# Eight groups of unread TensorE products taken out of the start of a two-layer gated network

## The reference, cut to what matters

```python
x = x + jnp.tanh(g_xattn[0]) * _L0_xattn_ref(_layernorm(x, axis=-1), fside_BxS2xS2_0, ctx_1024)
x = x + jnp.tanh(g_ffn[0]) * _L0_ffn_ref(_layernorm(x, axis=-1), L0_ffn_gate_w, ...)
x = x + jnp.tanh(g_xattn[1]) * _L1_xattn_ref(_layernorm(x, axis=-1), ctx_1024, L1_xattn_Wq, ...)
x = x + jnp.tanh(g_ffn[1]) * _L1_ffn_ref(_layernorm(x, axis=-1), L1_ffn_router_w, ...)
```

```python
amax_x = jnp.max(jnp.abs(x), axis=0)
amax_w = jnp.max(jnp.abs(w), axis=0)
s = jnp.sqrt(jnp.maximum(amax_x, EPS) / jnp.maximum(amax_w, EPS))
xs = x / s
ws = w * s
x_scale = jnp.maximum(jnp.max(jnp.abs(xs), axis=-1, keepdims=True), EPS) / QMAX
w_scale = jnp.maximum(jnp.max(jnp.abs(ws), axis=-1, keepdims=True), EPS) / QMAX
x_q = jnp.clip(jnp.round(xs / x_scale), -QMAX, QMAX)
w_q = jnp.clip(jnp.round(ws / w_scale), -QMAX, QMAX)
return x_q @ w_q.T * x_scale * w_scale.T
```

```python
gamma_w = jnp.clip(jnp.mean(jnp.abs(w)), 1e-05, None)
w_dq = jnp.clip(jnp.round(w / gamma_w), -1.0, 1.0) * gamma_w
```

## Time and profile before

| | |
|---|---|
| median of the runs | 465.94 us |
| profiled execution, its time | 466.42 us |
| profiled execution, span from the first to the last instruction | 464.6 us |
| TensorE busy | 418.9 us, 90% of the span |
| VectorE busy | 380.1 us, 82% |
| ScalarE busy | 349.7 us, 75% |
| GpSimd busy | 221.6 us, 48% |
| mean granted TensorE clock | 0.98 of full speed |

### The profile page before, as it was taken

One profiled execution on the slowest core, in us unless ns is written; L12 is line 12 of the kernel. 1 busy time (PEld: TensorE's weight loads), 2 busy tenths in 40 slices (PEclk: granted clock), 3 DMA queues, 4 the chain that ended last, 5 costly groups with the idle time before them and its releaser, 6 DMA issues.

```text
span 464.6 us, 7368 instructions
## 1 busy us (share of the span) xinstructions
PE 418.9 (90%) x2183; PEld 245.1 (53%) x2183; DVE 380.1 (82%) x955; ACT 349.7 (75%) x573; POOL 221.6 (48%) x343
## 2 busy tenths in 40 slices
PE   5866869979989987789999999999999999999986
PEld 4754657637646453335545545545554554554563
DVE  3799589999986887577898898889889889888853
ACT  1399867796999999657787777778778778776532
POOL 3285965776789555373333333424333333441220
PEclk9979889999999999989999999999999999999999
DMA  8999894358395902320231241232123123122101
GB/s 302 388 313 253 168 367 90 114 139 202 79 229 142 176 12 46 57 45 11 47 80 24 59 79 34 59 69 46 46 68 56 45 59 80 35 59 68 45 25 45
DMA packets 84952, 49.53 MB, mean 107 GB/s; under 512 B 70952, under 2 KB 73512, under 8 KB 83888
## 3 DMA queue, kind: packets, MB, share of 16 engines
q1 hardware_dynamic: 84912, 49.06, 41.2%
HBM read 28.33 MB, written 4.19 MB: 70 GB/s over the span
## 4 chain that ended last, share of the span: by engine, by line
PE 68%; DVE 8%; DMA 8%; ACT 5%; issue 4%; SPq 4%; POOL 3%; DVEq 0%; ACTq 0%; POOLq 0%
PE p_out L1825 11%; PE p_out L1913 11%; PE p_val L1818 11%; PE p_gate L1818 11%; DMA w_in<-in_fside_BxS2xS 4%; SPq L424 3%; PE p_tr L1800 3%; PE p_out L1847 3%; PE p_out L1873 3%; PE p_tr L1703 2%; DMA att_t<-in_L_ffn_val_w 2%; PE p_val L1783 2%; PE p_val L1769 2%; DMA att_t<-in_L_ffn_out_w 1%; PE p_val L1777 1%
## 5 line engine op out<-in xcount | busy, mean ns | idle before, releaser
L1818 PE MATMUL p_gate<-gate_t,q_room 128*128 128x512 fp8e4 x256 | 65.7, 379 | 1.3 <-ACT p_gate L1418 1.3
L1818 PE MATMUL p_val<-val_t,q_room 128*128 128x512 fp8e4 x256 | 65.7, 379 | 0.2 <-ACT p_val L1428 0.2
L1825 PE MATMUL p_out<-att_t,qT_room 128*128 128x512 f32 x120 | 57.1, 618 | 0.9 <-ACT qT_room L1244 0.9
L1913 PE MATMUL p_out<-out_t,ws_f 128*128 128x512 fp8e4 x240 | 54.4, 379 | 1.6 <-DMA ws_f<-ws_f 1.6
L611 POOL TENSOR_TENSOR rstd<-mv,ln_eps 128x1 f32<-128x1 f32 x48 | 9.2, 192 | 94.4 <-DVE mv L880 87.3
L1403 ACT ACTIVATE ctx_sb<-p_gate,bcol 128x512 f32<-128x512 f32 x64 | 43.7, 682 | 10.4 <-issue 7.3
L1418 ACT ACTIVATE p_gate<-w_slots,seed_scale 128x512 f32<-128x512 f32 x64 | 43.5, 682 | 9.9 <-POOL seed_scale L632 8.6
L909 DVE TENSOR_TENSOR act_f<-p_val,ctx_sb 128x512 f32<-128x512 f32 x64 | 44.1, 689 | 6.9 <-PE p_val L1818 5.4
L911 DVE TENSOR_REDUCE mu<-act_f 128x1 f32<-128x512 f32 x64 | 43.9, 686 | 2.2
L1428 ACT ACTIVATE p_val<-w_in,seed_scale 128x512 f32<-128x512 f32 x64 | 43.6, 680 | 0.1
L1818 PEld LDWEIGHTS p_val<-val_t,q_room 128*128 128x128 f16 x256 | 25.0, 98 | 30.7 <-ACT p_val L1428 0.9
(11 more groups left out here) (247 smaller groups left out, 982.2 us busy)
## 6 DMA issues: line engine op xcount, KB each, us to landing
att_t<-in_L_ffn_out_w SPq DMA_DIRECT2D x6, 1024.0 KB, 7.3
x_all<-in_x SPq DMA_DIRECT2D x4, 1024.0 KB, 8.9
att_t<-in_L_ffn_gate_w SPq DMA_DIRECT2D x4, 1024.0 KB, 13.1
out_dram<-x_all SPq DMA_DIRECT2D x15, 256.0 KB, 2.3
w_in<-in_fside_BxS2xS SPq DMA_DIRECT2D x3, 1024.0 KB, 7.6
att_t<-in_L_ffn_val_w SPq DMA_DIRECT2D x3, 1024.0 KB, 8.0
ctx_sb<-in_ctx SPq DMA_DIRECT2D x4, 512.0 KB, 5.2
side<-in_L_ffn_val_w SPq DMA_DIRECT2D x1, 1024.0 KB, 15.6
```

The source lines that it names most:

```text
L1818: last = nc.tensor.matmul(bank[:, c % 2, :], x_t[n % 2][:, k * P:(k + 1) * P], w_t[m][:, k, cols], start=False, stop=k == KD - 1, skip_gro ...
L1825: last = nc.tensor.matmul(p_out[:, 0, :], lt_c[:, k * P:(k + 1) * P], att_t[:, bass.ds((n // T) * (KD * S) + k * S, S)], start=k == 0, sto ...
L1913: last = nc.tensor.matmul(p_out[:, 0, :], p_t[:, k * P:(k + 1) * P], w_t[2][:, k, :], start=k == 0, stop=k == KH - 1)
```

## The change

The eight calls of `clock_raised` are taken out. All other lines, and the order of every other step on every engine, are as they were. The function itself stays, without a caller.

```diff
                 pe.wait_ge(consts_made, 12)
-                clock_raised(3)
-                clock_raised(2)
                 columns(0, 0, 1, 0)
...
                 columns(0, 0, 1, 3)
-                clock_raised(1)
-                clock_raised(0)
-                clock_raised(7)
                 columns(0, 0, 0, 0)
...
                 columns(0, 0, 0, 3)
-                clock_raised(6)
-                clock_raised(5)
                 rows(0, 0)
                 w_total(0)
                 w_transpose(0)
                 w_transpose(1)
                 w_transpose(2)
-                clock_raised(4)
                 columns(0, 1, 1, 0)
```

## The result

The changed kernel took 467.93 us in the median of 17 runs (465.29 to 471.11), the kernel before 465.71 us beside it (17 runs, 463.62 to 469.06). The ratio is 1.0051, 95% interval 1.0029 to 1.0072: half a per cent slower. Measured again later, in another set of runs, it was 466.89 us (12 runs) against 466.30 (35 runs), ratio 1.0014, interval 0.9986 to 1.0041. Taken over both sets, the mean of its 29 runs is 467.5 and that of the 122 runs of the kernel before (four sets) 466.1, or 0.3% less. The first set alone shows the changed kernel slower, the interval of the second holds no change too, and the best guess from both is 0.1 to 0.5% slower; each kernel scatters by some 1.1 to 2.1 us (standard deviation) about its mean.

A forecast was written before the change was run, and what follows sets the result against it. Bound: a chain woven from all engines until 65 us, through GpSimd's rounding and batch 2's `w_in`, then TensorE's loop. Start loss of +1.8 on 466.42 gave 468.2 profiled, 467.6 as median; range 465.3 to 469.1 us.

The forecast's parts named there:

- k = 3, 2 ahead of all: gain 0: At the very start: eight products leave, hidden by TensorE's 1.90 us wait for the `w_in` DMA; gain 0.
- k = 1, 0, 7: at most 0.33 back: Between `w_in` and `act_f` transposes: twelve products, 2.68 us, leave; VectorE is late next, so at most 0.33 us returns.
- The clock falls back, +0.5: From 12.6 to 15.4 us TensorE's clock falls; the other three `act_f` groups run low, ending 0.5 us later.
- `rows(0, 0)` low, gamma_w at 25.2 to 25.6: Without k = 6, 5 the wait before `rows(0, 0)` grows to 2.9 us; it takes 3.63, delaying `gamma_w` by 1.8.
- k = 4: 0, hidden by TensorE's wait for `w_in`: At 33 us four products leave; cost 0, covered by TensorE's 1.82 us wait at 63.49; without cover up to +1.5.
- The whole of it is handed on: From `gamma_w` through GpSimd's rounding, value loads and SyncE's queue to 63.45 us: the whole +1.8 us passes on.
- the likeliest case: The forecast itself: low clock at the start, +1.8 us handed on; own range 467.0 to 468.6 us, chance 0.50.
- rival A: At the start the clock holds or rises in time for `rows`: -0.3 us, 465.6; chance 0.20, including 0.10 clearly faster.
- B: Lost time is hidden between 24 and 63 us by DMAs or SyncE's queue: +0.3 to +0.8, say 466.5; chance 0.23.
- C: Clock still low at L1769's eight steps (67.79 us): up to 3.7 on top of 1.8, up to 471.4; chance 0.07.

The follow-up runs named there:

- the kernel with the two filled waits: Kernel before plus unread 512-column products in two later TensorE waits, seven ahead of columns(0, 2, 1, 0), six ahead of c_spread(0); 466.40 us, ratio 1.0011.

## Why the prediction came out right, step by step

1. *k = 3, 2 ahead of all: gain 0.* Not refuted by the time: with these alone 1.0011 (0.9975 to 1.0047). But "the transposes run at the lower level with them and without" holds for the transposes only. In the kernel before, and in that with k = 3, 2 alone, the clock was up after them. In the changed kernel's first profile it was not, in its second it was. In the kernel with the two filled waits it was not, although its start is that of the kernel before: there it came up at 15.0 only. Whether they make it more frequent isn't shown.

2. *k = 1, 0, 7: at most 0.33 back.* Right, and the trace shows why it was not even that: `act_f` started at 14.01 and VectorE was through with `w_in` at 15.43 as before.

3. *The clock falls back, +0.5.* The groups of `act_f` ran low, as forecast, and ended at 19.21 instead of 18.49: +0.7. But the clock did not fall back, it had never come up. In the second profile it did come up at about 12.1, and fell back behind one group of `act_f`, as the item says.

4. *`rows(0, 0)` low, gamma_w at 25.2 to 25.6.* Right: 21.40 and 3.79 for 21.2 and 3.63, `gamma_w` 25.44. The wait before it was 2.92, forecast 2.9. Eight products (or 16 transposes) in that wait bring `rows` back to 2.05, and the kernel with only the eight products is 2.3 us faster than the changed one in the same set. How much of this comes through `rows` is open, as said there.

5. *k = 4: 0, hidden by TensorE's wait for `w_in`.* This step failed, though its price is small: the cover that it named is not the one that counts. The groups of 44.1 to 47.4 ran low, GpSimd's `root(0, 1)` waits for them, and it came at 49.50 against 46.34, 3.2 us later where `gamma_w` was 2.0 later. With that L576 and L587 ended at 67.74 instead of 64.84, and VectorE's L831 had to wait for them, 1.27 us instead of 0.19. TensorE's wait at 63.5 was indeed still there (1.48 of 1.82), and says nothing on GpSimd. Of all this 0.3 us at most reached TensorE, between 76 and 78 us.

6. *The whole of it is handed on.* Half right. It arrived at the value loads (26.10 for 24.10, GpSimd's L543), but at 54.31 only 1.10 was left. The rows of SyncE's own queue show where it went: the eight issues L424 took 13.46 us from 39.71 before and 12.74 from 41.52 after. Behind ScalarE's last rounding the way to `x_load(3)` was 10.12 us before (43.09 to 53.21) and 9.09 after (45.22 to 54.31). I had seen no slack in that queue since the chain showed no idle step; single issues of 2.10, 1.71 and 1.60 us before, for 1.27 otherwise, were the slack. In the chain of the kernel before that ended last, the longest of them:

```profile
49.75 2.10 SPq L424
```

The longest of the changed kernel there is 1.36. Why they were longer isn't shown. The load of `w_in` for batch 2 took 0.3 us less, so TensorE had it at 64.25 and not at the 65.2 of the forecast.

*The sum.* +1.8 forecast, +1.9 in the profiled executions, +2.2 and +0.6 in the medians of the two sets. The agreement of the first two is partly luck: of the 1.9 about 1.0 is the start, and 0.86 is the slow tile of the loop, which no term of the sum had. The start was to hand on 1.8, so item 6 is too large by nearly half. The second median, 466.89, lies just below the likeliest case's own range (467.0 to 468.6), still inside the whole range of 465.3 to 469.1. That range starts 0.3 below the 465.6 that rival A's own sum gives.

*The rivals.* A (clock holds) did not come about in either profile of the changed kernel. The kernel with only k = 6, 5 gets a quick `rows`, though not a held clock, and that one is faster than the kernel before (0.9972). B (hidden) describes the second measurement, +0.6 us, better than my forecast does. C did not come about in either profile of the changed kernel: the eight steps of L1769 took 3.70 us, at 68.36 and at 66.91. It does exist: with only k = 1, 0, 7 they took 6.01, 2.3 us more. How often the changed kernel meets it isn't shown.

What was missing altogether is that the kernel before is itself no fixed point. Its 122 runs lie between 462.7 and 469.8. In each of the three sets of 35 the time goes with the mean granted clock of the run (correlation -0.76 to -0.83), so the low stretches go with a large part of the scatter. Which ones, isn't shown. That the unread products of the start run at either level, as the two executions of the same start show, is not enough: with twelve of them ahead of everything the runs scattered as widely. L1825 at 200 us, 3.70 or some 5.3 us by the level, and the waits for DMA transposes, up to 1.8 us, come into question as well.

## What to carry to other kernels

Work that only keeps the clock up is best put into a wait about as long as that work takes at the low clock, right ahead of work that is on the path (3.2 us in a wait of 2.9 here); between two pieces that are both ready it becomes the delay itself, whenever the clock happens to be low. Before pricing a low clock at nothing, follow every engine that reads TensorE's result, not only TensorE's own next wait. And a chain that shows no idle step can still give time back, in steps whose duration differs from that of their like. Last, follow a faster kernel's profile to its end before crediting the place that was changed: the one with only k = 6, 5 won its time at 190 to 206 us.

## What of the hardware was unexpected

- VectorE's TENSOR_SCALAR of 128x4 in SBUF takes 0.17 us alone and up to 1.27, 1.65, 2.17 or 2.54 us while GpSimd works, and ends within 0.1 us of the end of a GpSimd piece. The Trainium skill ("SBUF — State Buffer", section "SBUF: two separate sides") says that a VectorE instruction in a two-port mode and a GpSimd instruction exclude each other for a whole instruction. The ends agree with this, though no run shows in which mode L831 ran. But the 2.54 us reached past the end of GpSimd's L576 at 66.0 and to the end of L587, so the hold can outlast one instruction. VectorE's reductions, some of them beside the same GpSimd work (L829, 2.28 us), show no such stretch.
- Transposes alone bring the clock up: with nothing but transposes on TensorE since the start, 16 of them took 1.91 us at 18.16, where 15 took 3.39 us at 8.90 in the changed kernel.
- The same start met the clock's rise before 12.6 us in one execution and, worked out from 4.05 us for 24 records at 0.21 or 0.11 each, only at about 15 us in another. A single profile of such a kernel shows one draw; which level a stretch has should be read from more than one.
